# Eight and eight staging buffers in place of six and nine, with a new block order for the first sweep

## What is computed

```python
def reference(x, adj, ...):
    # L0: h @ W_self + (adj @ h / clip(rowsum(adj), 1)) @ W_neigh
    # L1: relu(adj @ (h @ kernel) + bias)
    # L2: relu(A @ (x @ W1) + b1), then relu(A @ (h @ W2) + b2)
    # L3: swish((adj @ x) @ W + b), then the same once more
    x = _layernorm(x + _L0_gnn_ref(x, adj, L0_gnn_W_self, L0_gnn_W_neigh), axis=-1)
    x = _layernorm(x + _L1_gnn_ref(x, adj, L1_gnn_kernel, L1_gnn_bias), axis=-1)
    x = _layernorm(x + _L2_gnn_ref(x, adj, L2_gnn_W1, L2_gnn_b1, L2_gnn_W2, L2_gnn_b2), axis=-1)
    x = _layernorm(x + _L3_gnn_ref(x, adj, L3_gnn_W, L3_gnn_b), axis=-1)
    return x
```

## Time and profile before

| | |
|---|---|
| median of 3 runs | 1139.68 us (1139.39 to 1141.41) |
| the profiled execution, its own time | 1139.4 us |
| its span, first to last instruction | 1137.4 us |
| PE busy | 1126.0 us (99%) |
| DVE busy | 840.0 us (74%) |
| ACT busy | 614.0 us (54%) |
| loads of `adj` | 515 of 512 KB and 2 of 256 KB |
| granted PE clock, all 40 slices | 9 tenths or more |

### The profile page before, as it was taken

How to read it: one execution, slowest core, us unless ns; L and a number is a source line. 1 busy time by engine, 2 the same in 40 slices (tenths; PEclk the granted TensorE clock), 3 DMA queues, 4 the chain that set the end, 5 groups by cost and what they waited for, 6 DMA issues and landing times.

```text
span 1137.4 us, 14378 instructions
## 1 busy us (share of the span) xinstructions
PE 1126.0 (99%) x5052; PEld 908.2 (80%) x5052; DVE 840.0 (74%) x1045; ACT 614.0 (54%) x857; POOL 80.8 (7%) x50
## 2 busy tenths in 40 slices
PE   8999999999999999999999999999999999999997
PEld 3557788888888888888888888888888888888886
DVE  6799999999897667684544498566677455677995
ACT  1257476566854444474444474444367445566884
POOL 0011011011131111000000010000000000000121
PEclk9999999999999999999999999999999999999999
DMA  9987777667968665596656487666658665797993
GB/s 345 339 296 258 255 258 225 211 231 232 310 218 292 199 208 207 175 369 204 206 186 216 171 294 283 215 202 207 222 200 324 213 205 188 251 325 278 337 320 117
DMA packets 82644, 278.42 MB, mean 245 GB/s; under 512 B 8848, under 2 KB 14480, under 8 KB 82576
## 3 DMA queue, kind: packets, MB, share of 16 engines
q1 hardware_dynamic: 76144, 272.86, 70.0%
q10 hardware_dynamic: 6432, 4.65, 1.5%
HBM read 275.38 MB, written 2.10 MB: 244 GB/s over the span
## 4 chain that ended last, share of the span: by engine, by line
PE 84%; DVE 7%; issue 3%; DMA 3%; ACT 2%; POOL 1%; ACTq 0%; POOLq 0%; DVEq 0%; SPq 0%
PE acc L503 24%; PE acc L504 24%; PE acc L508 24%; PE acc L491 7%; DVE deg_part L792 3%; PE acc L540 3%; DMA raw<-adj_tiles 3%; DVE adj_lo L925 2%; POOL rstd L952 1%; ACT t_x L698 0%; ACT t_x L721 0%; DVE op_lo L925 0%; ACT adj_hi L767 0%; PE acc L518 0%; PE acc L526 0%
## 5 line engine op out<-in xcount | busy, mean ns | idle before, releaser
L925 DVE TENSOR_TENSOR adj_lo<-raw,adj_hi 128x1024 fp32r<-128x1024 f32 x451 | 547.8, 1228 | 242.5 <-ACT adj_hi L767 227.2
L767 ACT CAST adj_hi<-raw 128x1024 fp32r<-128x1024 f32 x451 | 470.7, 1050 | 352.7 <-PE acc L508 264.4
L503 PE MATMUL acc<-adj_hi,op_hi 128*128 128x512 f32 x1400 | 551.4, 394 | 0.3 <-issue 0.3
L504 PE MATMUL acc<-adj_hi,op_lo 128*128 128x512 f32 x1400 | 545.3, 390 | 0.0
L508 PE MATMUL acc<-adj_lo,op_hi 128*128 128x512 f32 x1400 | 431.4, 389 | 0.0
L508 PEld LDWEIGHTS acc<-adj_lo,op_hi 128*128 128x128 f32 x1400 | 262.7, 188 | 55.5 <-DVE adj_lo L925 0.2
L503 PEld LDWEIGHTS acc<-adj_hi,op_hi 128*128 128x128 f32 x1400 | 263.0, 188 | 54.1 <-issue 1.2
L504 PEld LDWEIGHTS acc<-adj_hi,op_lo 128*128 128x128 f32 x1400 | 263.1, 188 | 53.6 <-issue 0.7
L792 DVE TENSOR_TENSOR deg_part<-deg_part,raw 128x1024 f32<-128x1024 f32 x112 | 136.7, 1220 | 6.8 <-DMA raw<-adj_tiles 4.9
L952 POOL TENSOR_TENSOR rstd<-var_eps,minus_half 128x4 f32<-128x4 f32 x31 | 66.8, 2156 | 1039.6 <-DVE var_eps L808 769.6
L491 PE MATMUL acc<-raw,x_rows 128*128 128x512 f32 x176 | 80.6, 611 | 4.2 <-DMA x_rows<-x_blocks 4.1
(11 more groups left out here) (79 smaller groups left out, 361.5 us busy)
## 6 DMA issues: line engine op xcount, KB each, us to landing
raw<-adj_tiles SPq DMA_DIRECT2D x515, 512.0 KB, 4.7
xt<-x_t ACTq DMA_DIRECT2D x8, 256.0 KB, 5.0
x_rows<-x_blocks SPq DMA_DIRECT2D x7, 256.0 KB, 5.9
out<-t_x ACTq DMA_DIRECT2D x7, 256.0 KB, 5.8
raw<-adj_tiles SPq DMA_DIRECT2D x2, 256.0 KB, 3.2
out<-xt SPq DMA_DIRECT2D x2, 128.0 KB, 1.8
x_rows<-x_blocks SPq DMA_DIRECT2D x1, 192.0 KB, 4.4
w<-W ACTq DMA_DIRECT2D x2, 64.0 KB, 4.7
```

Of the source, the lines that this page charges most:

```text
L503: nc.tensor.matmul(bank, op_block(op_hi, p, j), a_hi, start=first and b == 0, stop=False)
L504: nc.tensor.matmul(bank, op_block(op_lo, p, j), a_hi, start=False, stop=False)
L767: nc.scalar.copy(split_hi(s), raw[:, g % RAW, :]).then_inc(hi_ready, 1)
L925: nc.vector.tensor_tensor(split_lo(s), raw[:, g % RAW, :], split_hi(s).bitcast(fp32), ALU.subtract).then_inc(lo_ready, 1)
```

## The change

`RAW` goes from 6 to 8 and `SPLIT` from 9 to 8; a raw buffer is 4 KB of a partition and a split slot 8 KB, so that the space is the same. `FIRST_ORDER` is another order, again with 22 whole blocks; fewer of its blocks are FIRST/SECOND pairs. The tables that place the chains are set anew to fit. The computation is the same: 516 loads of steps, 768 products, 44 whole steps.

```diff
-    RAW = 6
-    SPLIT = 9
+    RAW = 8
+    SPLIT = 8
...
     FIRST_ORDER = [
-        (0, 0, 4, WHOLE), (0, 1, 4, WHOLE), (0, 0, 1, WHOLE), (0, 1, 1, WHOLE), (0, 0, 2, WHOLE), (0, 1, 3, WHOLE),
+        (0, 1, 1, WHOLE), (0, 0, 4, WHOLE), (0, 0, 7, WHOLE), (0, 0, 1, WHOLE), (0, 0, 5, WHOLE), (0, 1, 5, WHOLE),
...
     ROWS_AT = [
-        21, 31, 44, 58, 91, 110, 159, 170
+        21, 29, 50, 63, 96, 109, 140, 164
     ]
     DEGREES_AT = [
-        25, 38, 50, 83, 103, 133, 161, 176
+        23, 44, 53, 87, 102, 129, 157, 176
     ]
     WEIGHT_AT = [
-        26, 40, 53, 86, 105, 136, 165, 178, 194, 198, 202, 220, 238, 260, 278, 304, 318, 322, 326, 348, 366,
+        24, 46, 58, 91, 104, 135, 159, 178, 194, 198, 202, 220, 238, 260, 278, 304, 318, 322, 326, 348, 366,
...
     SELF_AT = [
-        213, 308, 389, 484, 661, 750, 990, 1046
+        197, 277, 438, 526, 694, 749, 918, 1013
     ]
     SUM_AT = [
-        214, 357, 438, 606, 718, 870, 982, 1053, 1190, 1222, 1254, 1326, 1406, 1502, 1582, 1678, 1782, 1814,
+        198, 390, 478, 646, 726, 862, 982, 1046, 1182, 1214, 1246, 1318, 1398, 1494, 1574, 1670, 1774, 1806,
...
     SCALE_AT = [
-        309, 390, 485, 662, 766, 910, 1052, 1126, None, None, None, None, None, None, None, None, None, None,
+        276, 446, 533, 702, 750, 934, 1014, 1118, None, None, None, None, None, None, None, None, None, None,
...
     OP_HI_AT = [
-        310, 398, 486, 670, 774, 918, 1054, 1134, 1253, 1270, 1286, 1366, 1446, 1534, 1614, 1734, 1806, 1838,
+        278, 454, 534, 710, 758, 942, 1022, 1126, 1245, 1262, 1286, 1358, 1438, 1526, 1606, 1726, 1798, 1837,
...
     OP_AT = [
-        286, 390, 478, 654, 774, 910, 1053, 1134, 1222, 1238, 1262, 1366, 1446, 1526, 1606, 1718, 1806, 1838,
+        270, 438, 510, 686, 750, 910, 1006, 1126, 1214, 1230, 1254, 1358, 1438, 1518, 1598, 1710, 1790, 1838,
```

More of the change, by code:

```diff
@@ L64, in bass_gnn_residual_norm_kernel @@
[L64 to L68, removed]
@@ L69, in bass_gnn_residual_norm_kernel @@
-        (0, 7, 2, FIRST), (0, 7, 4, SECOND), (0, 6, 6, ONE), (0, 6, 5, SECOND), (0, 6, 7, ONE), (0, 6, 3, FIRST),
-        (0, 7, 2, SECOND), (0, 7, 7, ONE), (0, 7, 0, BOTH), (0, 7, 5, BOTH), (0, 7, 6, FIRST), (0, 7, 1, FIRST),
-        (0, 6, 3, SECOND), (0, 7, 1, SECOND), (1, 3, 3, ONE), (1, 4, 4, ONE), (1, 2, 2, ONE), (0, 7, 6, SECOND)
+        (0, 1, 1, WHOLE), (0, 0, 4, WHOLE), (0, 0, 7, WHOLE), (0, 0, 1, WHOLE), (0, 0, 5, WHOLE), (0, 1, 5, WHOLE),
+        (0, 1, 0, WHOLE), (0, 0, 3, WHOLE), (0, 0, 0, WHOLE), (0, 0, 6, WHOLE), (0, 0, 2, WHOLE), (0, 1, 4, WHOLE),
@@ new lines, in bass_gnn_residual_norm_kernel @@
+        (0, 1, 2, ONE), (0, 2, 2, WHOLE), (0, 2, 3, ONE), (0, 1, 6, WHOLE), (0, 2, 7, WHOLE), (0, 2, 0, BOTH),
+        (0, 1, 7, WHOLE), (0, 2, 4, WHOLE), (0, 1, 3, ONE), (0, 2, 1, WHOLE), (0, 2, 6, WHOLE), (0, 3, 6, WHOLE),
+        (0, 3, 0, BOTH), (0, 2, 5, ONE), (0, 3, 5, ONE), (0, 3, 7, ONE), (0, 3, 1, BOTH), (0, 4, 1, BOTH),
+        (0, 4, 2, BOTH), (0, 3, 2, BOTH), (0, 4, 7, ONE), (0, 4, 0, BOTH), (0, 3, 3, ONE), (0, 3, 4, ONE),
+        (0, 4, 4, WHOLE), (0, 5, 2, BOTH), (0, 4, 6, ONE), (0, 4, 5, WHOLE), (0, 5, 1, BOTH), (0, 4, 3, BOTH),
@@ new lines, in bass_gnn_residual_norm_kernel @@
+        (0, 5, 0, FIRST), (0, 6, 2, BOTH), (0, 5, 3, BOTH), (0, 6, 0, FIRST), (0, 5, 4, BOTH), (0, 6, 0, SECOND),
+        (0, 5, 0, SECOND), (0, 5, 7, ONE), (0, 5, 6, ONE), (0, 5, 5, ONE), (0, 6, 6, ONE), (0, 6, 3, BOTH),
+        (0, 6, 7, ONE), (0, 6, 4, BOTH), (0, 7, 1, BOTH), (0, 6, 1, BOTH), (0, 7, 0, BOTH), (0, 6, 5, BOTH),
+        (0, 7, 5, BOTH), (0, 7, 2, BOTH), (0, 7, 6, FIRST), (0, 7, 7, ONE), (0, 7, 4, FIRST), (0, 7, 3, BOTH),
+        (1, 4, 4, ONE), (1, 2, 2, ONE), (0, 7, 4, SECOND), (1, 3, 3, ONE), (0, 7, 6, SECOND)
@@ L174, in bass_gnn_residual_norm_kernel @@
     ROWS_AT = [
[L175 removed]
+        21, 29, 50, 63, 96, 109, 140, 164
     ]
     DEGREES_AT = [
[L178 removed]
+        23, 44, 53, 87, 102, 129, 157, 176
     ]
     WEIGHT_AT = [
[L181 to L182 removed]
+        24, 46, 58, 91, 104, 135, 159, 178, 194, 198, 202, 220, 238, 260, 278, 304, 318, 322, 326, 348, 366,
+        388, 406, 432, 446, 450, 454, 476, 494, 516, 534, 560, 574, 578, 582, 604, 622, 644, 662, 702, 720, 726,
         732, 738, 742, 751, 762, 768
@@ L185, in bass_gnn_residual_norm_kernel @@
     X_HI_AT = [
-        205, 206, 207, 208, 209, 210, 211, 212
+        189, 190, 191, 192, 193, 194, 195, 196
     ]
     SELF_AT = [
-        213, 308, 389, 484, 661, 750, 990, 1046
+        197, 277, 438, 526, 694, 749, 918, 1013
     ]
     SUM_AT = [
[3 rows of a table removed]
[3 rows of a table added]
     ]
     SILU_AT = 32 * [None] + [
-        3054, 3092, 3118, 3214, 3294, 3389, 3470, 3710, 3854, 3902, 3958, 3997, 4030, 4078, 4129, 4132
+        3046, 3084, 3118, 3206, 3286, 3381, 3462, 3702, 3846, 3894, 3950, 3997, 4030, 4086, 4129, 4132
@@ L208, in bass_gnn_residual_norm_kernel @@
+        1870, 1958, 2038, 2134, 2214, 2310, 2454, 2494, 2518, 2606, 2686, 2774, 2854, 2974, 3053, 3086, 3126,
+        3214, 3294, 3382, 3470, 3710
     ]
     X_LO_AT = [
-        6, 38, 70, 86, 118, 150, 166, 182
+        6, 22, 38, 70, 102, 118, 150, 166
     ]
     RDEG_AT = [
-        214, 326, 414, 598, 694, 838, 982, 1054
+        198, 374, 446, 622, 694, 838, 958, 1054
     ]
     BIAS_AT = [
[3 rows of a table removed]
[3 rows of a table added]
     ]
     RESIDUAL_AT = 40 * [None] + [
-        3854, 3902, 3950, 3990, 4006, 4070, 4129, 4131
+        3846, 3894, 3942, 3982, 3998, 4062, 4129, 4131
@@ L222, in bass_gnn_residual_norm_kernel @@
     ]
     NORM_AT = [
[3 rows of a table removed]
[3 rows of a table added]
     ]
     OP_AT = [
-        286, 390, 478, 654, 774, 910, 1053, 1134, 1222, 1238, 1262, 1366, 1446, 1526, 1606, 1718, 1806, 1838,
-        1878, 1966, 2046, 2142, 2222, 2318, 2438, 2454, 2478, 2614, 2694, 2774, 2854, 2966, 3062, 3094, 3126,
-        3222, 3302, 3390, 3478, 3718
+        270, 438, 510, 686, 750, 910, 1006, 1126, 1214, 1230, 1254, 1358, 1438, 1518, 1598, 1710, 1790, 1838,
+        1870, 1958, 2038, 2134, 2214, 2310, 2430, 2454, 2486, 2606, 2686, 2766, 2846, 2958, 3054, 3086, 3126,
@@ L232, in bass_gnn_residual_norm_kernel @@
+        3214, 3294, 3382, 3470, 3710
     ]
     SCALED_AT = [
-        246, 358, 446, 630, 734, 886, 1022, 1086
+        230, 406, 502, 662, 741, 894, 998, 1078
     ]
     VAR_AT = [
-        254, 374, 462, 646, 749, 894, 1038, 1102
+        238, 422, 518, 678, 742, 917, 1006, 1094
     ]
```

6 lines of the change are left out of this document (removed), and 18 rows, old and new, of tables (BIAS_AT, NORM_AT, SCALE_AT, SUM_AT).

## The result

| | before | after |
|---|---|---|
| median, same chip, 12 runs each | 1140.45 us | 1138.34 us |
| lowest to highest | 1138.68 to 1144.17 | 1135.84 to 1141.13 |
| profiled execution | 1139.4 | 1138.63 |
| its span | 1137.4 | 1136.1 |

The ratio is 0.9978, interval [0.9968, 0.9987]: 0.22% faster, where no change was forecast. A later measurement of the same kernel gave 0.9972 [0.9959, 0.9984].

What follows compares the result with a forecast made beforehand. The prediction took PE, running at its matmul pace nearly everywhere, to bound the kernel. Gains of 2.1 us and a loss of 2.1 us at chunk 6's chain net to 0: 1139.7 us, range 1137.2 to 1142.7.

Steps and rivals of the forecast that it cites:

- Then the eight loads, 4.8 us (281.86 to 286.64), to 19.6: Chunk 6's chain on ACT: the weight loads follow the normalising, taking 4.8 us from t = 14.8, ahead of `op_hi`.
- t = 0: Start of product 157 on PE, from which the prediction timed chunk 6's chain on PE, ACT and DVE.
- The forecast of 2.1 us late at step 127: End of first sweep: low halves of steps 125, 126, 127 come 0.3, 1.2, 2.1 us late; PE loses about 2.1 us.
- my t = 12.1: When DVE was to reach the shift for chunk 6's normalised rows, which would then be there at 13.2.
- rival (b): The weight loads are hidden after all, so all gains of 2.1 to 2.4 us come: 1137.4 us, chance 0.20.
- The bound of 0: Lower bound of the loss at chunk 6's `op_hi` and `op_lo`: none if ACT reaches the loads 2.1 us earlier.
- late starts of 0.98, 0.20, 0.42, about 0.5 and 0.34 us: Five PE delays in chains between blocks, at 261.10, 288.24, 311.43, 325.62 and 1120.11 us; together 2.4, of which 2.1 counted.
- One split slot less: Costs one product, 1.36 us, of ACT's lead; priced at nothing, as PE has seven products, 9.5 us, in hand.
- More raw buffers: SP runs 8 steps ahead, not 6; at the first turn removes the 0.42 us and most of the 0.5.
- The second piece of x: A 256 KB load ahead of step 2, not step 4: bounds 0 and 0.76 us, taken as 0.
- (c): DVE falls behind PE in the middle of the first sweep, 2 to 4 us on top: 1142.7 us, chance 0.17.
- (d): Ring of eight split slots is short at the turns; 1 us at each of four makes 1143.7 us, chance 0.05.

Runs made afterwards that it cites:

- Experiment 7: Changed kernel with ACT waiting, ahead of the eight weight loads, until the normalised rows of chunk 6 are written: 1139.02 us, ratio 0.9991 to the kernel before.
- 12: Kernel before with the degree sums of chunk 6 two products later (163 in place of 161): 1140.26 us, ratio 1.0004.
- 13: Kernel before with chunk 6's degree sums two products later and the eight weight loads behind `op_hi`: 1139.9 us, ratio 1.0002.
- 5: The changed kernel measured again, nothing altered: 1136.26 us, ratio 0.9972 to the kernel before.
- 8: Kernel before with eight split slots in place of nine; six raw buffers and all tables as before: 1157.73 us, ratio 1.0158.
- 9: Kernel before with eight raw buffers and eight split slots, every table as before: 1155.66 us, ratio 1.0139.
- 1: Kernel before with eight raw buffers, eight split slots and the new tables for sweeps after the first; old first sweep kept: 1142.66 us, ratio 1.0023.
- 10: Kernel before with six raw buffers, eight split slots, old first sweep and the new tables for the later sweeps: 1152.94 us, ratio 1.0109 to the kernel before.
- 2: Changed kernel (new order and tables) with six raw buffers and nine split slots: 1164.87 us, ratio 1.0223 to the kernel before.
- 4: Changed kernel with eight more weight loads into a spare tile behind the eight: 1144.15 us, ratio 1.004 to the kernel before.
- 14: Kernel before with eight and eight buffers, old first sweep, newer later-sweep tables, and the eight weight loads behind `op_hi`: 1142.38 us, ratio 1.0017.
- 11: Changed kernel with seven raw buffers in place of eight: 1142.01 us, ratio 1.002 to the kernel before.

## Why the prediction was wrong

**The step that failed** is "Then the eight loads, 4.8 us (281.86 to 286.64), to 19.6". In the profile after, t = 0 of that sum is 255.22, 2.72 us ahead of the weight product of chunk 6. The loads begin at t = 13.0 and not 14.8, beside the normalising and not behind it, and `op_hi` begins at 17.1 and not 19.6. Of these 2.5 us, 1.5 are the overlap (268.26 to 269.73), 0.7 that it took 4.1 us and not 4.8 from the first load to `op_hi`, and 0.3 that the normalising began at 12.9 and not 13.2. The forecast of 2.1 us late at step 127, less 2.5, is 0.4 us of room, and 0.4 was measured.

Experiment 7 shows that the overlap decides. Without it `op_hi` begins at t = 18.3, 1.3 before the forecast, and 2.1 less 1.3 is the 0.8 by which step 127 was late. The 1.3 are 1.0 for quicker loads (3.8 us in 7) and the same 0.3. By the same sum the overlap with loads of 4.8 us would have left step 127 0.3 late; that is worked out, not tried. DVE reached its norm point 1.0 us before my t = 12.1, but ACT was then still at the rows of x until 268.1, so that this was worth no more than the 0.3.

This was rival (b), at a chance of 0.20, and it gave 1137.4. The bound of 0, with ACT at the loads 2.1 us earlier, comes near to what happened: 1.8 us earlier, and less time for them. That the measured gain of 2.1 us is that of (b) is in part luck, since the profile after also has late starts of 1.85 and 0.37 us that nothing in the prediction named. The Trainium skill ("DMA: Bandwidth & Descriptors", "Anatomy of one DMA — SWDGE (gpsimd) path") gives about 50 ns of dispatch for the path over GpSimd. That is not the price of these loads: each takes 0.33 to 0.64 us of ACT's sequencer in the profile after. What hid them was their place.

**The gains.** That the late starts of 0.98, 0.20, 0.42, about 0.5 and 0.34 us would go was right in every case. That each is worth its length was not a safe step: 12 and 13 took 0.98 out of the old order and got nothing, since ACT's chain and the raw data behind it set the next start. In the new order, where all five are gone at once, they do add up, as the next sum shows. Taking out some of them only was tried for the first alone.

**The rest of the sum.** Span 1137.4 less 2.4 of gains, plus 1.85 at the store and 0.37 at 126 us, is 1137.2; the trace has 1136.1. Of the 1.1 between them 0.7 lie at the very start: PE begins the fifth step of the program at 13.82 us and not at 14.51. This is not the change, since it differs as much from run to run: 13.2 to 14.6 us in the eight profiles of the old order, 13.4 to 14.1 in the eight of the new. In the profile of 5, which had neither loss, it is 13.53. The 1.0 from there, the 2.5 of the five late starts and some 0.2 for the matmuls behind them make 3.7 us, and the span is 3.65 shorter.

**The parts that I priced at nothing.** *One split slot less* was the largest error, though it did not show in the time of the change: with the old tables eight slots cost 16 to 18 us (8, 9), with the old first sweep alone 2.6 (1). My reason, seven products in hand, looked at the splits and not at what stands behind a split on ACT. *More raw buffers*: I gave them 0.42 and part of 0.5. Between six and eight of them lie 2 us with the old tables (8, 9), 10 with the old first sweep and the new tables behind it (10, 1), and some 28 under the new order, against a ninth slot (2). *The new tables*, which I took as following from the rest, are what makes eight slots possible. *The second piece of x* ahead of step 2 cost nothing that shows.

**The other rivals.** (c) did not happen: no low half was late in the middle of the sweep. (d), the ring short at a turn, is what experiment 1 shows for the old order, at one turn and with 2.5 us, where I had put 1 us and a chance of 0.05; the new order escapes it.

The measured time is inside the range. The forecast of no change missed a gain whose size is just what this kernel's measurement can tell.

## What to carry to other kernels

A slot fewer is not priced by how many products the consumer has in hand, but by what stands behind the instruction that waits for the slot on its engine. Sizes of rings and the order of instructions must be changed together: here each half of the change alone was slower (1.002 to 1.022) and both together faster. Before a DMA issue is added to a critical chain, look whether its sequencer may run it beside work already handed to the engine. And a late start is only worth its length if the next chain comes earlier too.

## What the runs showed of the hardware

- The same eight small loads took ACT's sequencer 3.8 us (7), 4.0 (after), 4.8 and 5.8 (12), with single issues from 0.33 to 2.07 us (12).
- ACT's sequencer issues loads while instructions ahead of them on ACT are still queued: after, three of four `t_x` and a split; with a wait for the four `t_x` ahead of the loads (7), the first load is issued at 269.21, when they are done (269.18).
- The same store took from 2.5 us (5) to 5.5 us (after) in the same place of the same program, and this alone moved the span by 1.9 us.
- After a stall of PE the granted clock can fall to 1.2 GHz. In 4, 3.1 us late were followed by 6.2 us at 0.51. In the new order with six and nine, windows of PE behind 2.3 us of idle time (columns: window, length, PE busy, granted clock, DMA share, GB/s):

```profile
187.10:192.30 5.20, 5.20 (x12) 0.50 0.54 180
193.00:200.00 7.00, 7.00 (x35) 1.00 0.54 173
```

The length of the stall alone does not say it: behind 1.68 us of idle time (after) the clock stayed at 1.00, behind 1.80 us (14) it was 0.66 over the next 4 us, and behind 1.93 us (9 and 11) it was 1.00 again.
